# A hybrid attention and expert block on one core: layernorm applied on ScalarE, the rotation's cosine part read from PSUM, SBUF work moved to GpSimd, other queue orders

## What is computed

```python
x = x + attn_a(layernorm(x))   # 8 sequences of 256 tokens, 32 heads, 8 kv heads, head size 16
x = x + ffn(layernorm(x))
x = x + attn_b(layernorm(x))   # the same shapes, other weights
x = x + ffn(layernorm(x))

def layernorm(x):  (x - mean(x)) / sqrt(var(x) + 1e-5)
def attn(x):       # rotary positions on q and k, causal softmax
    q, k, v = split(x @ w_qkv)
    q, k = rope(q), rope(k)                     # r1 = x1*cos - x2*sin; r2 = x1*sin + x2*cos
    return concat(softmax(mask(q @ k.T / 4)) @ v) @ w_o
def ffn(x):        # top 2 of 8 experts, LoRA of rank 16 on a shared base
    weights, selected = top_k(x @ gate_w.T, 2); weights = softmax(weights)
    return x @ base_w.T + base_b + 2 * sum_e(w_full[e] * (x @ A[e].T) @ B[e].T)
```

## Time and profile before

| | us |
|---|---|
| median of 3 runs | 820.34 (818.52 to 826.51) |
| the profiled execution, its own time | 823.84 |
| its span in the trace | 821.8 |
| TensorE / VectorE busy | 685.9 / 557.8 |
| GpSimd / ScalarE busy | 473.8 / 372.7 |
| mean granted TensorE clock | 0.90 of full speed |

### The profile page before, as it was taken

One profiled execution on the slowest core, in us unless ns is written; L12 is line 12 of the kernel. 1 busy time (PEld: TensorE's weight loads), 2 busy tenths in 40 slices (PEclk: granted clock), 3 DMA queues, 4 the chain that ended last, 5 costly groups with the idle time before them and its releaser, 6 DMA issues.

```text
span 821.8 us, 18302 instructions
## 1 busy us (share of the span) xinstructions
PE 685.9 (83%) x7498; PEld 513.9 (63%) x7498; DVE 557.8 (68%) x786; ACT 372.7 (45%) x554; POOL 473.8 (58%) x446
## 2 busy tenths in 40 slices
PE   5826788898988897897988899887988889888996
PEld 4715565775666666665667676665667766564574
DVE  4377484766768795876868697775869686467453
ACT  2324554644544453454536464543535453453521
POOL 1124384757657593755849385865858474673621
PEclk7955959898999999798999999998999998997899
DMA  9551726163453636255452625354452725444111
GB/s 335 111 150 48 158 65 139 60 145 115 95 152 73 161 88 166 83 126 162 92 161 63 167 86 137 127 101 139 91 163 54 175 68 114 110 96 109 41 52 52
DMA packets 49650, 95.14 MB, mean 116 GB/s; under 512 B 7936, under 2 KB 19840, under 8 KB 49568
## 3 DMA queue, kind: packets, MB, share of 16 engines
q1 hardware_dynamic: 49568, 93.98, 43.6%
HBM read 24.42 MB, written 10.49 MB: 42 GB/s over the span
## 4 chain that ended last, share of the span: by engine, by line
PE 44%; DVE 16%; issue 13%; DMA 8%; POOL 7%; ACT 6%; SPq 5%; DVEq 0%; POOLq 0%; ACTq 0%
PE PP L428 27%; PE PP L534 11%; DVE nm L1077 5%; ACT PT L929 4%; PE PP L520 3%; POOL PT L1237 3%; DVE R L231 3%; PE PP L441 2%; POOL NE L238 2%; DMA Qs<-R 2%; DVE XL L1038 1%; DVE tw L1134 1%; DVE xn L1064 1%; DMA QK<-Rh 1%; DMA QK<-R 1%
## 5 line engine op out<-in xcount | busy, mean ns | idle before, releaser
L1077 DVE TENSOR_REDUCE nm<-PP 128x4 f32<-128x1024 f32 (+1 forms) x192 | 228.6, 1215 | 74.8 <-PE PP L428 74.2
L1237 POOL TENSOR_SCALAR_AFFINE_SELECT PT<-PT 128x1024 f32<-128x1024 f32 x128 | 144.4, 1133 | 153.8 <-ACT PT L929 153.7
L929 ACT ACTIVATE PT<-PP 128x1024 f32<-128x1024 f32 x192 | 193.2, 1026 | 83.8 <-PE PP L520 83.0
L428 PE MATMUL PP<-QK 64*128 64x128 f32 (+1 forms) x1024 | 102.6, 310 | 39.7 <-DVE nm L1077 10.5
L534 PE MATMUL PP<-PT,V 128*32 128x512 f32 x768 | 110.8, 720 | 21.0 <-POOL PT L1237 19.2
L428 PEld LDWEIGHTS PP<-QK 64*128 64x128 f32 x1024 | 85.9, 212 | 55.0 <-issue 21.6
L428 PE MATMUL PP<-XH,WQh 64*128 64x256 f32 x768 | 95.7, 299 | 6.1 <-DVE XL L1038 5.0
L520 PE MATMUL PP<-QK 64*128 64x512 f32 x384 | 83.3, 444 | 9.4 <-ACT PT L929 3.0
L428 PE MATMUL PP<-XL,WQh 64*128 64x256 f32 x768 | 91.0, 287 | 0.0
L428 PE MATMUL PP<-XH,WQl 64*128 64x256 f32 x768 | 90.8, 286 | 0.0
L238 POOL TENSOR_TENSOR NE<-NE,NR 128x512 f32<-128x512 f32 x30 | 41.2, 1374 | 69.1 <-DMA NR<-sums 69.1
(11 more groups left out here) (99 smaller groups left out, 1297.4 us busy)
## 6 DMA issues: line engine op xcount, KB each, us to landing
QK<-Rh SPq DMA_DIRECT2D x64, 256.0 KB, 4.4
QK<-R SPq DMA_DIRECT2D x64, 208.0 KB, 3.9
QK<-R SPq DMA_DIRECT2D x64, 160.0 KB, 3.3
Qs<-R SPq DMA_DIRECT2D x32, 256.0 KB, 2.4
NR<-sums SPq DMA_DIRECT2D x64, 128.0 KB, 2.8
NE<-NE SPq DMA_DIRECT2D x32, 128.0 KB, 2.0
mid<-X SPq DMA_DIRECT2D x8, 512.0 KB, 5.4
X<-mid SPq DMA_DIRECT2D x8, 512.0 KB, 3.9
```

Source lines behind the costliest of these rows:

```text
L428: ins = e.matmul(t[:, k, c], lhs(rows, which[k]), rhs(rows, which[k]), start=start, stop=stop, skip_group_check=True)
L929: e.activation(PT[:, k % RING, :].rearrange("p (a x) -> p a x", a=2), PP[t][:, :, :], ACT.Exp, scale=0.25).then_inc(S["ex"], 1)
L1077: e.tensor_reduce(o, x, AX.X, ALU.max).then_inc(S["m"], 1)
L1237: e.affine_select(out=blk, in_=blk, compare_op=ALU.is_ge, fill=0.0, base=0, pattern=[[0, 8], [1, 128]], channel_multiplier=-1).then_inc(S[ ...
```

## The change

- **Layernorm.** `stats` on VectorE ends with mean and variance. A new `eps` on ScalarE makes variance plus epsilon and the negated mean (two instructions). `power` on GpSimd has a second instruction, `nb = -mean * rs`. `norm` is now in ScalarE's list: `xn = Identity(rs * X + nb)`.
- **Rotation.** `qe` copies to a buffer of its own, `Qf`, and no longer waits for the stores of the slot before. `rc` is now on VectorE only; it multiplies the PSUM tile with the cosine straight into `R` (all 1,024 query columns in one instruction, the 256 key columns in another), waits for `qe` and for those stores, and what frees the PSUM tile is now `rc`. `sw` swaps from `Qf`. `ra(2)`, `rl(1)` and `kl` are in GpSimd's list, the keys lie in `KL`'s place, and `kl` waits for one thing less.
- **Maxima.** `nm` has 16 columns in place of 128, `M2` transposes only these, and `mT` has one buffer, so `mc(p)` waits for `mr(p - 1)`.
- **Gates.** The difference of the two top gates is made inside the exp (as bias, one instruction for each tile, in place of a VectorE subtraction and one exp). `te` is apart from `gr`.
- **Weights.** `Wst` is 1,024 wide in place of 1,536.
- **All five lists have new orders**, the loads of the start among them. `load(1)` was the 11th transfer and is the 17th. `mu(14); power("f", 6)` of GpSimd is `power("f", 6); mu(14)`, and so for five of the six slots in which `mu` came first. Both `tr("f", ...)` of a slot stand ahead of the odd `PV` in the middle passes.

```diff
-        KV = sb("KV", [P, 2, 256], F32)
+        Qf = sb("Qf", [P, 6, 256], F32)
-        nm = sb("nm", [P, 2, 128], F32)
-        mT = sb("mT", [16, 2, 128], F32R)
+        nm = sb("nm", [P, 2, 16], F32)
+        mT = sb("mT", [16, 128], F32R)
...
-                cross(PP[t], 0, nm[:, p % 2, :]).then_inc(S["mt"], 1)
+                for k, rows in enumerate((UP, LO)):
+                    ins = e.transpose(PP[t][0:16, k, 0:64], nm[rows, p % 2, :], iden[rows, 64 * k:64 * k + 64])
+                ins.then_inc(S["mt"], 1)
...
             def qe(s, b, t):
                 if b < 2:
                     w.wait_ge(S["q01"], 8 * s + 8)
-                    for g in range(4):
-                        w.wait_ge(S[f"st{g}"], 48 * s)
-                    copy(R[:, 0:1024].bitcast(F32).rearrange("p (f x) -> p f x", f=2), PP[t][:, :, :]).then_inc(
-                        S["qe01"], 1)
+                    w.wait_ge(S["sw01"], 32 * s)
+                    copy(Qf[:, 0:4, :].rearrange("p (f c) t -> p f (c t)", f=2), PP[t][:, :, :]).then_inc(S["qe01"], 1)
...
+            def eps(c, s):
+                f = int(c == "f")
+                w.wait_ge(S["ng" + c], 2 * s + 2)
+                w.wait_ge(S["np" + c], 2 * s)
+                e.activation(ve_[:, f, :], mv[:, f, :, 1], ACT.Copy, bias=EPS).then_inc(S["ne" + c], 1)
+                e.activation(nme[:, f, :], mv[:, f, :, 0], ACT.Copy, scale=-1.0).then_inc(S["ne" + c], 1)
+
+            def norm(c, n):
+                f, i, s = int(c == "f"), n % 2, n // 2
+                w.wait_ge(S["np" + c], 2 * s + 2)
+                w.wait_ge(S[c + "t"], n)
+                e.activation(xn[:, f, :], X[:, 2 * (s % XR) + i, :], ACT.Identity, bias=nb[:, f, i:i + 1],
+                             scale=rs[:, f, i:i + 1]).then_inc(S[c + "xn"], 1)
...
+                if p:
+                    w.wait_ge(S[f"md{(p - 1) % 2}"], 16 * ((p + 1) // 2))
+                copy(mT[:, :].rearrange("r (f t) -> r f t", f=2), PP[t][0:16, :, 0:64]).then_inc(S["mc"], 1)
...
+                for i in range(2):
+                    e.activation(gx[:, i:i + 1], mx[:, i, 0:1], ACT.Exp, bias=mx[:, i, 1:2], scale=-1.0).then_inc(
+                        S["gx"], 1)
...
-                e.tensor_scalar(xn[:, f, :], X[:, 2 * (s % XR) + i, :], mv[:, f, i, 0:1], rs[:, f, i:i + 1], ALU.subtract,
-                                ALU.mult).then_inc(S[c + "xn"], 1)
...
+            def rc(s, b, t):
+                w.wait_ge(S["c_trig"], 16)
+                w.wait_ge(S["qe01" if b < 2 else "qe2"], s + 1)
+                for g in range(4):
+                    w.wait_ge(S[f"st{g}"], 48 * s)
+                if b < 2:
+                    e.tensor_tensor(QR.bitcast(F32), PP[t][:, :, :].rearrange("p f (c x) -> p (f c) x", c=2),
+                                    trig[:, 0, :].unsqueeze(1).to_broadcast([P, 4, 256]), ALU.mult).then_inc(S["rc01"], 1)
+                else:
+                    e.tensor_tensor(roped(2), PP[t][:, 0, 0:256].rearrange("p (q x) -> p q x", q=2), trigs(0, 2),
+                                    ALU.mult).then_inc(S["rc2"], 1)
...
                 e.tensor_tensor(rs[:, f, :], ve_[:, f, :], half[:, :], ALU.pow).then_inc(S["np" + c], 1)
+                w.wait_ge(S["np" + c], 2 * s + 1)
+                e.tensor_tensor(nb[:, f, :], nme[:, f, :], rs[:, f, :], ALU.mult).then_inc(S["np" + c], 1)
```

More of the change, by code:

```diff
@@ new lines, in _ @@
+            const("trig"); load(3); load(2); rows(1); rows(2); load(1); load(15); load(10); const("bias"); rows(3)
+            const("iota"); load(12); load(8); load(11); load(4); rows(4); load(9); qk(); sw(0, 0); sw(0, 2); st(0, 0)
+            st(1, 0); st(2, 0); st(3, 0); st(0, 1); st(1, 1); st(2, 1); st(0, 2); st(1, 2); st(3, 1); st(2, 2)
+            st(3, 2); sw(1, 0); sw(1, 2); wd(17); mr(0); mr(1); st(4, 0); st(4, 2); st(4, 1); mr(2); st(5, 2)
+            st(5, 0); st(5, 1); lc(0); mr(3); st(6, 1); st(6, 0); st(6, 2); rd(0); mr(4); xc(0); st(7, 0); st(7, 2)
@@ L411, in _ @@
+            rr(27); lc(28); xc(28); st(62, 2); st(62, 0); st(62, 1); rd(28); mr(60); rr(28); st(63, 1); st(63, 0)
+            st(63, 2); store(12); mr(61); lc(29); mr(62); xc(29); rd(29); rr(29); mr(63); lc(30); xc(30); rd(30)
+            lc(31); rr(30); xc(31); rd(31); rr(31); store(13); store(14); store(15)
             for i in range(2):
@@ new lines, in _ @@
+            ex(15, 1, 2); eps("f", 2); norm("f", 4); ex(15, 2, 3); norm("f", 5); qe(5, 0, 0); mc(16, 2)
+            high("f", 2, 1); oh(6); eps("a", 6); oe(7, 2); ex(16, 0, 1); ex(16, 1, 2); norm("a", 12); ex(16, 2, 2)
+            qe(5, 2, 3); mc(17, 1); norm("a", 13); ve(5, 1); fe(2, 0); high("a", 6, 2); rh(5); ex(17, 0, 0)
+            gate_exp(2); kh(5); ex(17, 1, 0); mc(18, 3); ex(17, 2, 2); oh(7); oe(8, 3); lora_high(2, 0); mc(19, 3)
+            ex(18, 0, 0); ex(18, 1, 3); ex(18, 2, 0); ex(19, 0, 3); ex(19, 1, 0); eps("f", 3); norm("f", 6)
@@ new lines, in _ @@
+            ex(40, 2, 1); ve(11, 0); mc(41, 3); fe(8, 2); norm("a", 25); rh(11); high("a", 12, 1); gate_exp(8)
+            ex(41, 0, 0); kh(11); ex(41, 1, 2); ex(41, 2, 1); mc(42, 0); oh(19); oe(20, 0); lora_high(8, 2)
+            mc(43, 0); ex(42, 0, 0); ex(42, 1, 2); ex(42, 2, 0); ex(43, 0, 2); ex(43, 1, 1); eps("f", 9)
+            norm("f", 18); ex(43, 2, 1); norm("f", 19); qe(12, 0, 0); mc(44, 3); oh(20); high("f", 9, 2)
+            eps("a", 13); oe(21, 3); ex(44, 0, 2); ex(44, 1, 3); norm("a", 26); ex(44, 2, 3); qe(12, 2, 1); mc(45, 2)
@@ L1028, in _ @@
+            lora_high(13, 3); high("f", 14, 1); fe(14, 3); eps("f", 15); gate_exp(14); norm("f", 30); norm("f", 31)
+            lora_high(14, 0); high("f", 15, 2); fe(15, 3); gate_exp(15); lora_high(15, 2)
         @block.vector
@@ new lines, in _ @@
+            rl(3, 1); kl(3); causal(9, 0); causal(9, 2); gt(0); mu(3); fH(0); ol(3); causal(10, 0); causal(10, 2)
+            causal(11, 0); power("f", 1); causal(11, 2); mu(4); addbias(1); ol(4); causal(12, 0); power("a", 5)
+            rs_(4, 1); rs_(4, 0); rs_(4, 2); ra(4, 0); ra(4, 2); causal(12, 2); ra(4, 1); kl(4); causal(13, 0)
+            rl(4, 0); rl(4, 1); causal(13, 2); mu(5); gt(1); fH(1); ol(5); causal(14, 0); causal(14, 2)
+            causal(15, 0); power("f", 2); mu(6); causal(15, 2); addbias(2); ol(6); power("a", 6); rs_(5, 1)
@@ new lines, in _ @@
+            causal(16, 0); rs_(5, 0); ra(5, 1); ra(5, 0); causal(16, 2); rs_(5, 2); ra(5, 2); rl(5, 0); rl(5, 1)
+            kl(5); causal(17, 0); causal(17, 2); gt(2); mu(7); fH(2); ol(7); causal(18, 0); causal(18, 2)
+            causal(19, 0); power("f", 3); mu(8); causal(19, 2); addbias(3); ol(8); power("a", 7); rs_(6, 1)
+            causal(20, 0); rs_(6, 0); ra(6, 1); ra(6, 0); causal(20, 2); rs_(6, 2); rl(6, 0); ra(6, 2); rl(6, 1)
+            causal(21, 0); kl(6); gt(3); causal(21, 2); fH(3); mu(9); ol(9); causal(22, 0); causal(22, 2)
```

1029 lines of the change are left out of this document (492 added, 537 removed).

## The result

The changed kernel takes 743.44 us (median of 4 runs, 741.46 to 747.37), the one before in the same job 819.43 (813.58 to 826.51). The ratio is 0.910, with an interval of 0.903 to 0.917. I had forecast 794, with a range from 776 to 818. The direction was right, and the gain was nearly three times what I had worked out: 76 us and not 26. The profiled run took 747.37 us, its span is 745.4.

What follows compares the result with a forecast made beforehand. TensorE's work plus its gaps, from mu's round-trip wait and late VectorE, was taken as the bound; -13 + 4 - 10 - 8 - 1 + 1.5 = -26.5 us gave 794 us, range 776 to 818.

Steps and rivals of the forecast that it cites:

- TensorE's work plus the gaps in it: Whole kernel: no engine is full; mu's wait for the row sums' round trip and late VectorE make TensorE's gaps.
- `qe` and the rotation ... I take 0: Query copy: its wait for the stores only moves from ScalarE to VectorE's rc; 0 us.
- The orders: Passes where mu stood ahead of the f-norm power: f-norms no longer follow mu; 2 us in five passes, 10 us gained.
- VectorE, 13 us: VectorE loses norm applies and key work; two thirds of the 19.5 us nm gaps gained, bounds 4 and 22.
- ScalarE, +4: ScalarE gains norm applies and small instructions, which may delay exps: 0.3 us a pass, 4 us lost, bounds 0 and 15.
- GpSimd, 0: GpSimd loses rc, gains key work: 30.1 to 31.4 us a pass, nothing charged.
- The start, -8: Start: 5.7 us from the rotation, 2.3 from the mask copy, together 8 us gained, bounds 2 and 12.
- TensorE's 686 little changed: Sign that the forecast is right: TensorE's busy time stays near 686 us.
- rival B: Gaps close further and cold PV steps go too, 15 us more: sum -41, 779 us; chance 0.18.
- A: Rival: the row sums' round trip sets the pass, gains ahead of it are waited off at mu; 809 us, chance 0.16.
- C: Rival: GpSimd's queue from even mu to the last causal block becomes the chain, slower at 838 us; chance 0.12.
- D: Rival: norm applies waiting at the head of ScalarE's queue hold exps, 1 us a pass; 807 us, chance 0.14.

Runs made afterwards that it cites:

- e4: Changed kernel with the reciprocal row sums' way back cut (NR read early from the input for 28 head pairs): 735.26 us, 8 less.
- e6: Kernel before the change with the same cut of the reciprocal row sums' way back: 815.81 us, ratio 1.0002.

## Why the prediction was wrong, point by point

**What bounds it.** "TensorE's work plus the gaps in it" holds. The step that failed is the next: I took the waits that end last in the trace as the ones that set the pass, `mu` for `NR` in one half and VectorE in the other. The cut of the round trip gave 0 us before (the earlier trace rows had 69.1 us of it). Another wait stood right behind, the copy's for the stores, and it was this one that the copy, and with it the pass, kept to. The two terms that this step mis-sized are the copy's (0, measured 47) and VectorE's (13, measured 34); undone together they give 77 us.

**"`qe` and the rotation ... I take 0"** is the term that was wrong, by 47 us. My reason was that the same stores end the wait, on ScalarE or on VectorE. They do: VectorE's `rc` waited 12.9 us for them in all, and TensorE 5.9 us for `rc`. These are the rows of the changed kernel (L1103 is `rc` of the queries, L1106 of the keys):

```profile
DVE R L1103 <- DMA QK<-R: 6.0, 6, 2.4
DVE R L1106 <- DMA QK<-R: 6.9, 2, 4.0
PE PP L424 <- DVE R L1103: 3.2, 1, 3.2
PE PP L424 <- DVE R L1106: 2.7, 2, 2.1
```

But on ScalarE the copy has `mc`, the swap on SP and, behind the swap, `mr` after it, and in the new lists `oh` too; on VectorE `ra` and a PSUM tile that TensorE takes again hang on `rc`, and what stands behind it in VectorE's queue. I looked at who is idle and not at who stands behind, which the prediction did for `mu` and left out here. That there was 47.5 us of such waiting on ScalarE was in the trace of before, and is not in the rows that I chose. TensorE's own waits hide it: they have only 8.1 us in 3 for `R` from ScalarE.

**The orders.** I costed them by the place of the f-norms alone, 10 us. The runs show that nothing was to be had from the instructions without them (19 us more than before in the old orders with all of them, 16 with norms and keys left on VectorE). `qe` ahead of `mc` and `oh` was in the change, and I had not read it out of the lists. How much of the whole belongs to "the orders" has no number: it is not a sum, each needs the other.

**VectorE, 13 us.** By its edit it is 34: 24 for the norms and 14 for the keys, a little less together. About 6 of it lie in the start, where I had not looked for it. What I bounded at 22 were the `nm` gaps alone, and they fell by 12.2. What I had not counted is that `xn` itself was behind on VectorE. I had put its 19.2 us down to `mu` ahead of the f-norm.

**ScalarE, +4.** Its busy time was forecast near 430 us and is 433.4. The price of an apply was wrong, and the row for it is this:

```profile
L902 ACT ACTIVATE xn<-X,nb,rs 128x512 f32<-128x512 f32 x64 | 51.9, 812 | 18.2 <-POOL nb L1250 11.4 <-PE PP L437 6.6
```

It is 812 ns, and the copy's row gave 624. The estimate from the Trainium skill (ScalarE: Activation LUTs, "What ACT_TABLE_LOAD costs", on the `ACTIVATE` instruction), 0.80 us, agrees with this row. What the 12 us more of work cost was not tried by itself. ScalarE has over 300 us idle, and with the norms on it TensorE waits 11.2 us for `xn`, less than with them on VectorE (30.4).

**GpSimd, 0.** Its busy time was forecast near 495 us and is 469.6. `kl` came to 1.04 and 0.81 us, near the 1.9 together that I took. What I had too high were the larger ones: 1.31 us for `rl` where the row of before had 1.41. `mu` went from 1.374 to 1.278. I had set the rule of the Trainium skill (GPSIMD Engine Reference, "Engine selection") aside by one row, the 1.16 us of a `kl` of 256 columns on VectorE. On VectorE and in the new layout (the run with only the keys moved back) the same subtraction takes 0.68 us, and `rl` 0.76 against 1.31 on GpSimd:

```profile
L214 DVE TENSOR_TENSOR R<-R,Rh 128x512 fp32r<-128x512 f32 x15 | 11.5, 764 | 0.0
L228 DVE TENSOR_TENSOR R<-R 128x256 fp32r<-128x256 f32 x14 | 9.5, 676 | 0.0
```

These means are 1.7 and 1.2 times. The price that I held against the rule, 1.16 us, was not VectorE's own: by single instructions (last section) the subtraction of 256 columns takes 0.42 us with GpSimd idle beside it, against 0.73 us on GpSimd with VectorE idle, and the one of 512 columns 0.68 against 1.29 us. So the trace agrees with the rule, with 1.7 and 1.9 times. The move still gave 14 us, so the length of the one instruction did not decide.

**The start, -8.** `PV(0)` comes 7.1 us earlier and the first `Rh` at 34.70 us, which I had near 38. The size was right, in part by luck. I had put 5.7 us down to the rotation and 2.3 to the mask copy. But with the norms back on VectorE `PV(0)` comes 5.7 and 6.4 us later and the first `Rh` at about 40 us; with the old load order it is 3.6 and with the copy waiting again 2.7 us later. The norms in the start had no term. `load(1)` as the seventeenth transfer did no harm that shows.

**The clock.** "TensorE's 686 little changed" was wrong by 23 us. With fewer gaps ahead of `PV` the granted clock in its 20 steps from `PV(4)` on went from 0.81 to 0.94, and a step from 3.62 us to 3.04. Over all 768 matmuls it is 15.1 us (110.8 to 95.7), the size that my rival B has for it:

```profile
L531 PE MATMUL PP<-PT,V 128*32 128x512 f32 x768 | 95.7, 634 | 13.8 <-POOL PT L1259 11.1
```

B was the rival nearest to the result, with 0.18. For the gaps it named the transposes ahead of `PV`, and it was the copy. Nor is a faster `PV` a gain by itself: in the kernel before without the round trip it is 19.8 us shorter (91.0), and the time is the same.

**The rivals.** A (the round trip sets the pass) is out by `e4` and `e6`. C (GpSimd's queue) didn't come. D is not borne out: in the new orders the norms on ScalarE are worth 24 us, and in the old ones a run without them there is slow as well. For the end I had +1.5 us. Behind `PV(30)` it is 6.7 us more, 5.3 of them TensorE's work, as the new order leaves it 508 matmuls there in place of 464; its gaps grow by 1.4.

**The bounds.** The bounds of my terms, added up, give -48.5 and +10.5 us, and not the -45 and -8 that I wrote. The measured -76 lies outside them either way: the copy had no bounds of its own, and VectorE's upper bound was 22.

**What stays open.** Of the 76 us the two undone edits explain all, by size, but they were measured in the new orders. Why the new orders with both undone are no better than the old ones was not tried. By the table their A is 0.9 us shorter than before (22.0) and their B 1.8 us longer (25.8).

## What to carry to other kernels

Before a wait is put at nothing because "the same event ends it elsewhere", list what stands behind it in its queue and behind those in the next; here that same wait cost 47 us on ScalarE, while TensorE waited only 5.9 us for what VectorE did behind it. A long wait in the trace, such as the 69.1 us at `mu`, is not a gain to be had: look for the next wait that ends at the same place, or divide the loop at a few marks and see which part a change moves. In this kernel the freed queue paid in the new written orders and not in the old ones, so undo the parts in the new order, and try them alone in the old one.

## What I had not expected of the hardware

The same subtraction of 256 columns took 1.16 us on VectorE before and 0.68 us in the run with the keys on VectorE. Both are means of two kinds. Read one by one from the timelines, it takes 0.41 to 0.42 us wherever GpSimd is idle beside it (3 times before, 6 in that run). In the kernel before, 11 of the 16 ran beside an instruction of GpSimd with two inputs, and these took 0.42 to 1.51 us, 1.34 on average. Two from the kernel before, the second beside GpSimd's `mu`:

```profile
120.12 0.41 DVE L231 TENSOR_TENSOR R<-KV,R 128x256 fp32r<-128x256 f32 x1
...
208.92 1.61 POOL L238 TENSOR_TENSOR NE<-NE,NR 128x512 f32<-128x512 f32 x1
209.31 1.51 DVE L231 TENSOR_TENSOR R<-KV,R 128x256 fp32r<-128x256 f32 x1
```

It goes both ways. GpSimd's product of 512 columns `NE` with `NR` went from 1.374 to 1.278 us though nothing in it was edited. In the kernel before it took 1.26 us in the 12 cases with VectorE idle beside it, and 1.57 us on average in the 6 beside an instruction of VectorE with two inputs. The norm apply on VectorE shows it too: 0.54 us in the 33 cases with GpSimd idle, 1.07 us on average in the 24 beside a two-input instruction of GpSimd. The 1.60 us of the earlier trace rows is one of these. The reduction of the maxima, which reads PSUM, took 1.21 to 1.22 us on average either way. No run tried this by itself; it is how single instructions of the traces fall into groups.
